# One added VectorE sum in place of a second ones product for key group 3, its product moved behind the next q/k product, and GpSimd's bias passes moved in its order

## The chip, the cores and the metric

The kernel runs on one core of a Trainium2 chip. The metric is the device time in microseconds (us) of one execution; lower is better. TensorE multiplies matrices, VectorE and ScalarE work on up to 128 partitions elementwise, GpSimd (POOL in the rows) is a third elementwise engine, SyncE issues most of the transfers (DMA). Each engine runs its own list of instructions in order and waits on semaphores for the others.

## The reference, cut to what matters

A decoder layer over a batch of 16 sequences, 256 positions, 512 channels, all in float32:

```
x = _layernorm(x + attention(x))          # 16 heads of 32, softmax over the keys, low-rank updates folded into the weights
x = _layernorm(x + x * scan(ctx * ctx))   # a decaying sum over positions: r = d * r + ctx * ctx
x = _layernorm(x + ffn(x))                # rms_norm, 8-bit activations, ternary weights, 512 -> 2048 -> 512
# inside the ffn: silu, gelu, layer_norm with gain and bias, then quantised again
```

The softmax needs, for each head and query, the sum of exp(score) over the 256 keys. The kernel gets it as a product of the exponentials with a block of ones, beside the product with the values.

## The kernel before

The 16 batches are software-pipelined. Each engine has a lead, then `body(j)` for j = 1 to 15, then a drain. `body(j)` holds work on several batches: attention of batch j (four groups c = 0 to 3 of four heads each), the output product, first two layer norms and first FFN product of batch j-1, the middle of the FFN (gelu, norm, gain, bias, quantisation: called z) of batch j-2, the second FFN product and last norm of batch j-3. The names end in their batch: `quantise_z(j - 2, 0)` works on the first half (q = 0) of the 256 positions of batch j-2. The order inside a body is written out by hand per engine, and the semaphore counts in `table` join the engines.

What the change and the steps of the prediction touch:

- Attention. `probs` (128 keys x 2 key halves x 4 heads x 256 queries, float32) is written by ScalarE in `probs_of(b, c)` (L657, two instructions). TensorE's `weighted(b, c)` makes the product with the values (L1406, 16 small matmuls) and the product with `ones` (L1415, 16 matmuls, for c = 1 to 3). For c = 0, VectorE adds the two key halves first (`add_halves`, L979, into `half_sum`, which lies over `x_round`), and the ones product has 8 matmuls (L1411). VectorE's `attn_norm(b, c)` (L993 to L1002) waits for `pv_ready`, the count of finished ones products, and divides. `maxima` (L963) reduces the scores to maxima.
- z path. GpSimd `h_rstd` (L534 to L540), ScalarE `h_norm` (L740), GpSimd `g_mul` (L549, the gain), VectorE `z_add` (L1094, the bias), `z_max` (L1099) and `quantise_z` (small steps L1117 to L1123, then the large L1126), ScalarE `zq_store` (L710). Behind `zq_store(j - 2, 0)` in ScalarE's list come the eight `silu` of batch j-1 (L719), which empty the PSUM banks of TensorE's first FFN product `f(j, u)`, u = 0 to 7 (L1482 and L1483). Three banks take turns, so `f(j, 3)` waits for the first `silu`. After the eighth come two `gelu` (L725), the next body's `probs_of(j, 0)`, `h_var` (L735) and `h_norm`.
- Scan. VectorE `scan(j)` (L1010, four instructions of 128x256, then L1013) is the last item of VectorE's body.
- GpSimd's bias passes. `res1(b)` (L498, two of 128x512) adds the output bias to the rows of x, `res2(b)` (L507, the same size) the FFN's. Both stand at the head of GpSimd's body: `res1(j - 1)`, `res2(j - 2)`, `neg_mean` (L527) twice, `inverse_std3`, `h_rstd`.
- `normalise(3, b, q)` (L695) is ScalarE's last norm of a batch before it is stored. SyncE's body: load xT, `transpose_z(j - 3, 1)`, `store_out(j - 3, 0)`, `load_ctx`, `transpose_x(j - 1)`, `store_out(j - 3, 1)`, `transpose_z(j - 2, 0)`, `load_rows(j)`.

Of the kernel before, what the change touches and what calls it, by code (L numbers as in the profile page):

```python
# [12 lines left out]
ALU = mybir.AluOpType  # L13
# [4 lines left out]
T = 256  # L18
# [29 lines left out]
def decoder_kernel(nc, x, xT, ctxT, W, L, bq, bk, bv, bo, decay, w1T, b1, ln_g, ln_b, w2T, b2, out):  # L48
    b1_scratch = nc.dram_tensor("b1_scratch", (NPART, INNER), BF16, kind="Internal").ap()

    with ExitStack() as ctx:
# [70 lines left out]
        def sem(name):  # L122
# [40 lines left out]
            (PE, "shiftT_ready", 4), (PE, "pv_ready", 4), (PE, "o_ready", 2), (PE, "rT_ready", 2),  # L163
# [8 lines left out]
            (DV, "half_added", 1), (DV, "qk_lo", 8), (DV, "max_done", 4), (DV, "shift_split", 8), (DV, "inverted", 12), (DV, "attn_done", 4),  # L172
# [101 lines left out]
        def _(sp):  # L274
# [83 lines left out]
            def body(j):  # L358
# [6 lines left out]
                transpose_x(j - 1)  # L365
                if alive(j, 3):
                    store_out(j - 3, 1)
                if alive(j, 2):
                    transpose_z(j - 2, 0)
                load_rows(j)  # L370
# [38 lines left out]
        def _(po):  # L409
# [162 lines left out]
            attn_split(0, 3)  # L572

            def body(j):
                if alive(j, 1):
                    res1(j - 1)
                if alive(j, 2):
                    res2(j - 2)
                    neg_mean(j - 2, 0)
                    neg_mean(j - 2, 1)  # L580
# [27 lines left out]
                if alive(j, 2):  # L608
                    z_rms(j - 2, 1)

            def drain():
                res1(LAST)
# [32 lines left out]
        def _(ac):  # L645
# [162 lines left out]
            def body(j):  # L808
# [54 lines left out]
                if alive(j, -1):  # L863
                    v_store(j + 1, 0)
                if alive(j, 0):
                    probs_of(j, 3)
# [4 lines left out]
                if alive(j, 3):  # L871
                    normalise(3, j - 3, 1)
# [71 lines left out]
        def _(dv):  # L944
# [30 lines left out]
            def add_halves(b):  # L975
# [3 lines left out]
                dv.tensor_tensor(half_sum, probs[:, 0, :, :], probs[:, 1, :, :], ALU.add).then_inc(S["half_added"], 1)  # L979

# [206 lines left out]
            def lead():  # L1187
# [28 lines left out]
                maxima(1, 0)  # L1216
                attn_norm(0, 3)
# [5 lines left out]
            def body(j):  # L1223
# [42 lines left out]
                if alive(j, 2):  # L1266
                    z_add(j - 2, 1)
                    quantise_z(j - 2, 0)
# [54 lines left out]
        def _(pe):  # L1323
# [72 lines left out]
            def weighted(b, c):  # L1396
# [6 lines left out]
                for kt in range(NT):  # L1403
                    for i in range(GH):
                        ch = (GH * c + i) * HD
                        pe.matmul(bank[4][i * HD:(i + 1) * HD, 0:T], v_sb[b % 2][:, kt, ch:ch + HD], probs[:, kt, i, :],  # L1406
                                  start=(kt == 0), stop=(kt == NT - 1))
                if c == 0:
                    wait(pe, "half_added", b, 1)
                    for i in range(GH):  # L1410
                        last = pe.matmul(bank[4][i * HD:(i + 1) * HD, T:2 * T], ones[:, :], half_sum[:, i, :],  # L1411
                                         start=True, stop=True)
                for kt in range(NT if c > 0 else 0):
                    for i in range(GH):
# [314 lines left out]
```

## Time and profile before

| | |
|---|---|
| median of 3 runs | 1043.13 us (1042.7 to 1046.71) |
| the profiled execution | 1045.01 us, its span 1043.2 us |
| clock granted to TensorE over the span | 0.961 of full speed |
| core of the pipeline | bodies 3 to 15, a batch each 57.6 us |
| lead and first bodies | up to about 224 us of the span |
| drain | from about 960 us |

The span is the stretch between first and last instruction in the profile. A row of a timeline gives start, duration, engine, line, operation, what it writes and reads, and in brackets how long the engine sat idle just before, and for whom. The chain of waits follows the work that ended last back from the end. "issue" in it is time in which the profile shows nothing that the engine waited for.

### The profile page before, as it was taken

How to read it: one execution, taken by the hardware profiler on the slowest of the kernel's cores; microseconds unless marked ns; L12 is line 12 of the kernel's file. 1: busy time of each engine (PE TensorE's matmuls, PEld its weight loads, DVE VectorE, ACT ScalarE, POOL GpSimd, SP SyncE). 2: the span in 40 equal slices, each digit the busy share in tenths (PEclk: the TensorE clock that was granted, in tenths of full speed). 3: DMA queues.
4: the chain of work that ended last, by engine and by line, in shares of the span. 5: the costliest groups of instructions: out<-in, count | busy, mean ns of one | idle time of the engine just before them, and what ended most of it. 6: DMA issues, size and time to landing. Idle time of an engine off the chain costs nothing.

```text
span 1043.2 us, 23326 instructions
## 1 busy us (share of the span) xinstructions
PE 945.8 (91%) x9260; PEld 647.9 (62%) x9260; DVE 909.1 (87%) x1490; ACT 827.8 (79%) x957; POOL 582.7 (56%) x767
## 2 busy tenths in 40 slices
PE   4898897999999999999999999999999999977415
PEld 3776656676776667676767767676767777654102
DVE  5577878999999999999999999999999999996766
ACT  3556686888889797988989797989889897978684
POOL 3322338374765748484747658484747566572653
PEclk8899998999999999999999999999999999999768
DMA  9423100313122122323132121323131222122214
GB/s 361 156 87 137 43 33 21 74 34 99 25 58 70 49 75 52 84 52 85 21 85 52 55 62 52 84 52 85 52 85 22 71 61 58 42 52 63 53 33 90
DMA packets 106351, 73.67 MB, mean 71 GB/s; under 512 B 91385, under 2 KB 91385, under 8 KB 104450
## 3 DMA queue, kind: packets, MB, share of 16 engines
q1 hardware_dynamic: 105522, 70.34, 24.7%
q8 instruction: 74, 1.21, 0.5%
q10 hardware_dynamic: 720, 1.84, 0.5%
q14 instruction: 35, 0.29, 0.1%
HBM read 41.73 MB, written 8.40 MB: 48 GB/s over the span
## 4 chain that ended last, share of the span: by engine, by line
DVE 32%; PE 29%; ACT 16%; issue 13%; POOL 7%; DMA 3%; SPq 1%; DVEq 0%; ACTq 0%; POOLq 0%
PE bank L1343 9%; PE bank L1482 8%; DVE neg_max L963 6%; POOL h L549 5%; ACT h L725 3%; DVE h L1094 3%; DVE stats L1020 3%; ACT junk L735 2%; ACT h L740 2%; DVE qk_parts L986 2%; DVE fz L1099 2%; PE bank L1483 2%; PE wave L1392 2%; ACT L725 2%; PE wave L1368 2%
## 5 line engine op out<-in xcount | busy, mean ns | idle before, releaser
L963 DVE TENSOR_REDUCE neg_max<-wave 128x8 f32<-128x2048 f32 x64 | 146.1, 2282 | 20.0 <-PE wave L1368 20.0
L549 POOL TENSOR_TENSOR h<-h,g_tile 128x2048 f32<-128x2048 f32 x30 | 139.8, 4660 | 39.1 <-ACT h L740 39.1
L657 ACT ACTIVATE probs<-wave 128x1024 f32<-128x1024 f32 x128 | 124.3, 1024 | 37.8 <-PE wave L1392 37.7
L1482 PE MATMUL bank<-w,xqT 128*128 128x512 fp8e4 x496 | 130.0, 385 | 15.8 <-DMA xqT<-xq 13.0
L439 POOL TENSOR_SCALAR attn_hi<-attn 128x256 fp32r<-128x256 f32 x64 | 28.1, 439 | 176.4 <-DVE attn L1002 161.5
L695 ACT ACTIVATE rows<-rows,rstd 128x512 f32<-128x512 f32 x96 | 74.3, 807 | 41.1 <-POOL rstd L455 23.6
L1094 DVE TENSOR_TENSOR h<-h,b_tile 128x2048 f32<-128x2048 f32 x32 | 84.1, 2630 | 18.6 <-POOL h L549 18.0
L719 ACT ACTIVATE h<-bank,qx 128x512 f32<-128x512 f32 x124 | 82.3, 689 | 19.8 <-PE bank L1483 17.8
L498 POOL TENSOR_TENSOR rows<-rows,bo_tile 128x512 f32<-128x512 f32 x32 | 57.2, 1809 | 71.6 <-DMA rows<-x 71.6
L1489 PE MATMUL bank<-w,hqT 128*128 128x512 fp8e4 x416 | 94.3, 380 | 0.5 <-DMA hqT<-h 0.5
L1482 PEld LDWEIGHTS bank<-w,xqT 128*128 128x128 bf16 x496 | 46.6, 99 | 74.7 <-DMA xqT<-xq 9.9
L1010 DVE TENSOR_TENSOR_SCAN ctx_sb<-decay_col,ctx_sb 128x256 f32<-128x256 f32 x64 | 89.5, 1457 | 0.0
L1343 PE MATMUL bank<-xT_hi,wq_hi 128*128 128x256 f32 x256 | 77.8, 304 | 0.1
L1392 PE MATMUL wave<-qk_parts 32*128 32x256 f32 x1536 | 74.2, 302 | 3.8 <-ACT shift_rows L679 3.8
L442 POOL TENSOR_TENSOR attn_lo<-attn,attn_hi 128x256 fp32r<-128x256 f32 x64 | 73.5, 1148 | 5.3
L740 ACT ACTIVATE h<-h,fs 128x2048 f32<-128x2048 f32 x32 | 66.8, 2090 | 10.8 <-POOL fs L540 10.8
L672 ACT ACTIVATE qk_parts<-bank,bias_qk 128x256 fp32r<-128x256 f32 x128 | 53.6, 474 | 25.4 <-PE bank L1343 25.4
L1406 PE MATMUL bank<-probs,v_sb 128*32 128x256 f32 x1024 | 70.9, 396 | 3.1 <-ACT probs L657 2.1
L1392 PEld LDWEIGHTS wave<-qk_parts 32*128 32x128 f32 x1536 | 57.5, 190 | 25.8 <-issue 18.9
L1368 PE MATMUL wave<-qk_parts 32*128 32x256 f32 x1536 | 63.8, 297 | 10.1 <-ACT probs L657 8.0
L1343 PE MATMUL bank<-xT_lo,wq_hi 128*128 128x256 f32 x256 | 72.8, 284 | 0.0
L1343 PE MATMUL bank<-xT_hi,wq_lo 128*128 128x256 f32 x256 | 72.6, 284 | 0.0
(184 smaller groups left out, 2817.9 us busy)
## 6 DMA issues: line engine op xcount, KB each, us to landing
ctx_sb<-ctxT SPq DMA_DIRECT2D x16, 512.0 KB, 3.7
rows<-x SPq DMA_DIRECT2D x16, 512.0 KB, 4.0
out<-rows SPq DMA_DIRECT2D x32, 256.0 KB, 2.5
xT_in<-xT SPq DMA_DIRECT2D x15, 512.0 KB, 4.7
h<-w1T SPq DMA_DIRECT2D x4, 1024.0 KB, 14.3
h<-w2T SPq DMA_DIRECT2D x4, 1024.0 KB, 4.8
h<-Wq SPq DMA_DIRECT2D x1, 1024.0 KB, 6.0
h<-Wk SPq DMA_DIRECT2D x1, 1024.0 KB, 9.7
```

The source lines that it names most:

```text
L549: po.tensor_tensor(h_of(b, q)[:, :], h_of(b, q)[:, :], g_tile[:, :], ALU.mult).then_inc(done, 1)
L657: ac.activation(probs[:, kt, :, :], wave[:, :, kt * T:(kt + 1) * T], ACT.Exp, scale=SM_SCALE).then_inc(S["probs_ready"], 1)
L719: ac.activation(h_of(b, q)[:, n * FW:(n + 1) * FW], bank_of("f", u, b), ACT.Silu, scale=qx[:, X_DEQ, q:q + 1]).then_inc(S["silu_done"], 1)
L740: ac.activation(h_of(b, q)[:, :], h_of(b, q)[:, :], ACT.Identity, scale=fs[:, q, H_RSTD:H_RSTD + 1], bias=fs[:, q, H_NB:H_NB + 1]).then_in ...
L963: dv.tensor_reduce(neg_max[:, :, :], wave[:, :, :].rearrange("p j (t k) -> p j t k", t=NT), axis=AX_X, op=ALU.max, negate=True).then_inc(S ...
L1010: dv.tensor_tensor_scan(ctx_sb[:, c, :], decay_col[:, c:c + 1].to_broadcast([P, T]), ctx_sb[:, c, :], 0.0, ALU.mult, ALU.add).then_inc(S[" ...
L1094: dv.tensor_tensor(h_of(b, q)[:, :], h_of(b, q)[:, :], b_tile[:, :], ALU.add).then_inc(S["z_added"], 1)
L1343: last = pe.matmul(psum, lhsT, rhs, start=(first and i == 0), stop=(final and i == len(pairs) - 1))
L1368: last = pe.matmul(bank[head][:, qt * T:(qt + 1) * T], parts[at, qp, qt * P:(qt + 1) * P], parts[at, kp, :], start=(i == 0), stop=(i == 2))
L1392: last = pe.matmul(bank[head][:, kt * T:(kt + 1) * T], keys, queries, start=(i == 0), stop=(i == 3))
L1482: pe.matmul(p[:, :], xqT[:, q, kc, :], w1[:, kc, n * FW:(n + 1) * FW], start=(kc == 0), stop=False)
L1489: last = pe.matmul(p[:, :], hqT[:, k, :], w2[:, k, :], start=(k == 0), stop=(k == FC - 1))
```

## The change

- `weighted(b, 3)` makes only the product with the values, and counts it on a new semaphore `values_ready`. VectorE's new `add_in_place(b)` waits for it, adds `probs[:, 0]` to `probs[:, 1]` in place, 128x1024 float32, and counts `half_added`. The ones product of group 3, `summed(b, 3)`, then has 8 matmuls where it had 16, and stands behind `qk(j + 1, 1)`. Groups 0 to 2 keep their products and their places.
- `add_in_place(j)` stands in VectorE's body between `z_add(j - 2, 1)` and `quantise_z(j - 2, 0)`.
- On GpSimd `res1(j)` moves to the end of body j, behind a wait for `shift_split` of batch j+1 (its first `maxima`). `res2(j - 2)` now waits for the scan of batch j-1, behind `neg_mean(j - 2, 0)`.
- On ScalarE `normalise(3, j - 3, 1)` moves up, ahead of `probs_of(j, 3)`. On SyncE `store_out(j - 3, 1)` moves ahead of `transpose_x(j - 1)` and `load_rows(j)` ahead of `transpose_z(j - 2, 0)`.

```diff
--- before.py
+++ after.py
@@ -160,7 +160,7 @@
         table = [
 
             (PE, "shifted_ready", 4), (PE, "scores_ready", 4), (PE, "qk_ready", 4), (PE, "v_ready", 2),
-            (PE, "shiftT_ready", 4), (PE, "pv_ready", 4), (PE, "o_ready", 2), (PE, "rT_ready", 2),
+            (PE, "shiftT_ready", 4), (PE, "pv_ready", 4), (PE, "values_ready", 1), (PE, "o_ready", 2), (PE, "rT_ready", 2),
             (PE, "f_ready", 8), (PE, "y_ready", 2),
 
             (AC, "probs_ready", 8), (AC, "v_stored", 2), (AC, "x_hi", 1), (AC, "qk_hi", 8),
@@ -169,7 +169,7 @@
             (AC, "xq_stored", 1), (AC, "silu_done", 8), (AC, "zq_stored", 2),
             (AC, "gelu_done", 2), (AC, "h_var", 2), (AC, "h_normed", 2), (AC, "z_squared", 2),
 
-            (DV, "half_added", 1), (DV, "qk_lo", 8), (DV, "max_done", 4), (DV, "shift_split", 8), (DV, "inverted", 12), (DV, "attn_done", 4),
+            (DV, "half_added", 2), (DV, "qk_lo", 8), (DV, "max_done", 4), (DV, "shift_split", 8), (DV, "inverted", 12), (DV, "attn_done", 4),
             (DV, "scan_done", 5), (DV, "ln1", 6), (DV, "ln2", 6), (DV, "x_quant", 14),
             (DV, "z_added", 4), (DV, "z_quant", 12),
             (DV, "ln3", 6),
@@ -362,12 +362,12 @@
                     transpose_z(j - 3, 1)
                     store_out(j - 3, 0)
                 load_ctx(j)
-                transpose_x(j - 1)
                 if alive(j, 3):
                     store_out(j - 3, 1)
+                transpose_x(j - 1)
+                load_rows(j)
                 if alive(j, 2):
                     transpose_z(j - 2, 0)
-                load_rows(j)
 
             def drain_transpose(b, q):
 
@@ -570,13 +570,13 @@
             attn_split(0, 1)
             attn_split(0, 2)
             attn_split(0, 3)
+            res1(0)
 
             def body(j):
-                if alive(j, 1):
-                    res1(j - 1)
-                if alive(j, 2):
+                if alive(j, 2):
+                    neg_mean(j - 2, 0)
+                    wait(po, "scan_done", j - 1, 5)
                     res2(j - 2)
-                    neg_mean(j - 2, 0)
                     neg_mean(j - 2, 1)
                 if alive(j, 3):
                     inverse_std3(j - 3, 0)
@@ -607,9 +607,11 @@
                     attn_split(j, 3)
                 if alive(j, 2):
                     z_rms(j - 2, 1)
+                if alive(j, -1):
+                    wait(po, "shift_split", j + 1, 2)
+                res1(j)
 
             def drain():
-                res1(LAST)
                 neg_mean(PRIOR, 0)
                 neg_mean(PRIOR, 1)
                 inverse_std1(LAST)
@@ -862,14 +864,14 @@
                     shiftT(j, 3)
                 if alive(j, -1):
                     v_store(j + 1, 0)
+                if alive(j, 3):
+                    normalise(3, j - 3, 1)
                 if alive(j, 0):
                     probs_of(j, 3)
                 if alive(j, 1):
                     xq_store(j - 1)
                 if alive(j, -1):
                     v_store(j + 1, 1)
-                if alive(j, 3):
-                    normalise(3, j - 3, 1)
                 if alive(j, 0):
                     ctx_square(j)
                 if alive(j, 2):
@@ -978,6 +980,13 @@
                 wait(dv, "xq_stored", b - 2, 1)
                 dv.tensor_tensor(half_sum, probs[:, 0, :, :], probs[:, 1, :, :], ALU.add).then_inc(S["half_added"], 1)
 
+            def add_in_place(b):
+
+                wait(dv, "probs_ready", b, 8)
+                wait(dv, "values_ready", b, 1)
+                dv.tensor_tensor(probs[:, 1, :, :], probs[:, 0, :, :], probs[:, 1, :, :],
+                                 ALU.add).then_inc(S["half_added"], 1)
+
             def qk_lo(b, c):
 
                 wait(dv, "qk_hi", b, 2 * (c + 1))
@@ -1214,6 +1223,7 @@
                 attn_norm(0, 2)
                 ternary(1)
                 maxima(1, 0)
+                add_in_place(0)
                 attn_norm(0, 3)
                 qk_lo(1, 1)
                 ternary(2)
@@ -1265,6 +1275,8 @@
                     quantise_x(j - 1)
                 if alive(j, 2):
                     z_add(j - 2, 1)
+                add_in_place(j)
+                if alive(j, 2):
                     quantise_z(j - 2, 0)
                 if j == 1:
                     ternary(7)
@@ -1403,17 +1415,26 @@
                 for kt in range(NT):
                     for i in range(GH):
                         ch = (GH * c + i) * HD
-                        pe.matmul(bank[4][i * HD:(i + 1) * HD, 0:T], v_sb[b % 2][:, kt, ch:ch + HD], probs[:, kt, i, :],
-                                  start=(kt == 0), stop=(kt == NT - 1))
-                if c == 0:
-                    wait(pe, "half_added", b, 1)
+                        last = pe.matmul(bank[4][i * HD:(i + 1) * HD, 0:T], v_sb[b % 2][:, kt, ch:ch + HD],
+                                         probs[:, kt, i, :], start=(kt == 0), stop=(kt == NT - 1))
+                if c == 3:
+                    last.then_inc(S["values_ready"], 1)
+                else:
+                    summed(b, c)
+
+            def summed(b, c):
+
+                if c in (0, 3):
+                    wait(pe, "half_added", b, 1 if c == 0 else 2)
+                    both = half_sum if c == 0 else probs[:, 1, :, :]
                     for i in range(GH):
-                        last = pe.matmul(bank[4][i * HD:(i + 1) * HD, T:2 * T], ones[:, :], half_sum[:, i, :],
+                        last = pe.matmul(bank[4][i * HD:(i + 1) * HD, T:2 * T], ones[:, :], both[:, i, :],
                                          start=True, stop=True)
-                for kt in range(NT if c > 0 else 0):
-                    for i in range(GH):
-                        last = pe.matmul(bank[4][i * HD:(i + 1) * HD, T:2 * T], ones[:, :], probs[:, kt, i, :],
-                                         start=(kt == 0), stop=(kt == NT - 1))
+                else:
+                    for kt in range(NT):
+                        for i in range(GH):
+                            last = pe.matmul(bank[4][i * HD:(i + 1) * HD, T:2 * T], ones[:, :], probs[:, kt, i, :],
+                                             start=(kt == 0), stop=(kt == NT - 1))
                 last.then_inc(S["pv_ready"], 1)
 
 
@@ -1600,6 +1621,7 @@
                 scores(1, 0)
                 weighted(0, 3)
                 qk(1, 1)
+                summed(0, 3)
                 shiftT(1, 0)
                 shifted(1, 0)
 
@@ -1663,6 +1685,7 @@
                     weighted(j, 3)
                 if alive(j, -1):
                     qk(j + 1, 1)
+                summed(j, 3)
                 if j == 1:
                     pe.wait_ge(u_tern, 4)
                     pe.wait_ge(u_b1_in, 16 * NPART)
```

## Rows read from the trace of the kernel before

**Rows 1.** The page's busy time, share of the span and instructions of each engine.
```profile
PE 945.8 (91%) x9260; PEld 647.9 (62%) x9260; DVE 909.1 (87%) x1490; ACT 827.8 (79%) x957; POOL 582.7 (56%) x767
```

**Rows 2.** One batch's stretch: length, busy PE, PEld, DVE, ACT, POOL, clock, DMA.
```profile
627.20:684.80 57.60, 57.05 (x579) 39.48 (x578) 53.61 (x90) 49.34 (x59) 36.12 (x48) 1.00 0.25 62
```

**Rows 3.** Chain of waits, 627 to 687 us: start, us, what.
```profile
627.31 1.84 DVE h L1094
...
654.22 1.30 DVE h L1126
655.57 2.00 issue
659.60 1.04 PE bank L1482 x4
...
674.59 1.98 ACT junk L735 x2
678.04 2.11 ACT h L740
680.22 4.69 POOL h L549
684.93 1.80 DVE h L1094
```

**Rows 4.** Timeline of VectorE, 593 to 630 us.
```profile
593.44 2.29 DVE L1094 TENSOR_TENSOR h<-h,b_tile 128x2048 f32<-128x2048 f32 x1
595.65 0.15 DVE L1117 TENSOR_TENSOR fz<-fz 128x1 f32<-128x1 f32 x1
...
607.80 6.66 DVE L1010 TENSOR_TENSOR_SCAN ctx_sb<-decay_col,ctx_sb 128x256 f32<-128x256 f32 x4
...
618.24 1.21 DVE L979 TENSOR_TENSOR x_round<-probs 128x1024 f32<-128x1024 f32 x1
619.37 2.28 DVE L963 TENSOR_REDUCE neg_max<-wave 128x8 f32<-128x2048 f32 x1
...
627.31 2.48 DVE L1094 TENSOR_TENSOR h<-h,b_tile 128x2048 f32<-128x2048 f32 x1 [1.38 <-POOL h L549]
```

**Rows 5.** Who waited for whom: us in total, times, longest.
```profile
DVE h L1094 <- POOL h L549: 18.0, 13, 1.4
```

**Rows 6.** Timeline of ScalarE: body 2, then 597 and 647 us.
```profile
196.38 1.28 ACT L719 ACT_TABLE_LOAD   x1 [0.32 <-PE bank L1483]
...
597.99 2.00 ACT L710 ACTIVATE h<-h,neg_round 128x2048 bf16<-128x2048 f32 x1 [0.22 <-DVE h L1126]
...
647.48 1.95 ACT L657 ACTIVATE probs<-wave 128x1024 f32<-128x1024 f32 x2 [0.51 <-PE wave L1392]
```

**Rows 7.** Timeline of TensorE, 594 to 620 us.
```profile
594.56 1.05 PE L1415 MATMUL bank<-probs,ones 128*32 128x256 f32 x16
...
602.05 1.04 PE L1482 MATMUL bank<-w,xqT 128*128 128x512 fp8e4 x4 [0.17 <-ACT h L719]
...
619.89 0.61 PE L1411 MATMUL bank<-x_round,ones 128*32 128x256 f32 x8
```

**Rows 8.** Timeline of GpSimd, 599 to 620 us.
```profile
599.58 0.40 POOL L439 TENSOR_SCALAR attn_hi<-attn 128x256 fp32r<-128x256 f32 x1 [8.47 <-DVE attn L1002]
...
606.81 3.84 POOL L498 TENSOR_TENSOR rows<-rows,bo_tile 128x512 f32<-128x512 f32 x2 [5.11 <-DMA rows<-x]
610.61 3.30 POOL L507 TENSOR_TENSOR rows<-rows,b_tile 128x512 f32<-128x512 f32 x2
...
619.08 0.42 POOL L534 TENSOR_SCALAR fs<-fs 128x1 f32<-128x1 f32 x1 [1.01 <-ACT junk L735]
```

**Rows 9.** All instructions of L1010 and of L498: ns minimum/median/maximum.
```profile
L1010 DVE TENSOR_TENSOR_SCAN ctx_sb<-decay_col,ctx_sb x64: 659/1693/1784, 86.8 to 951.4; 128x256 f32<-128x256 f32 x64
...
L498 POOL TENSOR_TENSOR rows<-rows,bo_tile x32: 1261/1656/2350, 79.8 to 953.9; 128x512 f32<-128x512 f32 x32
```

**Rows 10.** Timeline of VectorE in the lead, 80 us.
```profile
80.07 0.87 DVE L986 SCALAR_TENSOR_TENSOR qk_parts<-bank,bias_qk,qk_parts 128x256 fp32r<-128x256 f32 x2 [1.49 <-ACT qk_parts L672]
```

## The prediction, made before the changed kernel ran

> **What bounds the kernel now.** I read the page's busy shares first. TensorE is busy 945.8 us of the span and VectorE 909.1 [rows 1], which names two candidates and decides nothing. The view by stretches comes next. A batch of the steady part takes 57.60 us, and in it TensorE is busy 57.05, VectorE 53.61, ScalarE 49.34 and GpSimd 36.12 [rows 2]. TensorE has half a microsecond of air, so a loop that is longer than 57.05 and runs through several engines must set the period. The chain of waits shows it [rows 3]. The reader is to see the same item, `z_add` of the first half (L1094), at 627.31 and again at 684.93, 57.62 us later, and what lies between.
>
> First comes a stretch of VectorE alone, from `z_add(j-2, 0)` at 627.31 to the end of `quantise_z(j-2, 0)` (L1126) at 655.5, some 28.2 us. Then the chain leaves VectorE: `zq_store` on ScalarE (the 2.00 us called issue at 655.57), a table load, the first `silu`, TensorE's `f(j, 3)` at 659.60 and the four after it, the last `silu`, both `gelu`, `probs_of`, `h_var` at 674.59, GpSimd's `h_rstd`, `h_norm` at 678.04, `g_mul` of 4.69 us, and again `z_add` [rows 3]. Each joint is tight. `zq_store` started 0.22 us after it was free, on VectorE's L1126 [rows 6]. `f(j, 3)` came after 0.17 us of idle TensorE, on the first `silu` [rows 7]. `h_rstd` came after 1.01 us of idle GpSimd, on `h_var` [rows 8]. `z_add(j-2, 0)` came after 1.38 us of idle VectorE, on `g_mul` [rows 4], and that wait occurs 13 times, 18.0 us in all [rows 5].
>
> So VectorE's list falls into two parts of unlike value. Between `z_add(j-2, 0)` and `quantise_z(j-2, 0)` each microsecond is a microsecond of the period. Between `quantise_z(j-2, 0)` and the next `z_add` (last group's division, `maxima`, scan, norms, `add_halves`) VectorE has 1.38 us in hand, and time saved there only lengthens the wait for `g_mul`.
>
> **The change part by part.**
>
> The new sum on VectorE. It stands between `z_add(j-2, 1)` and `quantise_z(j-2, 0)`, in the part without slack. Its twin is `add_halves` (L979), the same 128x1024 float32 with both inputs in SBUF: 1.21 us, and the next item starts 619.37 - 618.24 = 1.13 us after it [rows 4]. The neighbours here overlap in the same way (L1094 of 2.29 us, next start 2.21 later), so I take 1.13. That it writes over an input isn't shown by any row; I see no work removed or added by it. What it waits for has happened: `z_add(j-2, 1)` ends at 595.7, and the product with the values ends just after 594.6, where the ones product starts [rows 4, 7]. Behind it wait `quantise_z`, and through it `zq_store`, all eight `silu` and TensorE's `f(j, 3)`. ScalarE is free before L1126 ends [rows 6], so nothing covers it: +1.13 a batch, at most 1.21.
>
> The ones product on TensorE. 16 matmuls took 1.05 us [rows 7], 8 take 0.61: 0.44 saved in front of `f(j, 0)`, and `qk(j+1, 1)` starts some 0.9 earlier. It lies ahead of `f(j, 3)`, which waits for the first `silu`. TensorE's idle time of 0.17 there becomes 0.17 + 0.44 + 1.13 = 1.74 us. Worth nothing while the loop binds. `summed(j, 3)` needs the sum at about 596.9 and TensorE reaches it after `qk` at 597.5, so no stall. `f(j, 2)` uses the bank of the last group's division, which is now 1.13 later, near 600.7, about where `f(j, 2)` stood: a few tenths, ahead of the same wait.
>
> GpSimd's passes and the scan. Beside the bias passes (3.84 and 3.30 us) the scans took 6.66 us [rows 4, 8]. Over all batches one scan has a minimum of 0.66 and a median of 1.69, one bias pass a minimum of 1.26 and a median of 1.66 [rows 9]. With the passes gone I expect 4 x 0.66 less overlap, some 2.4 to 2.6 us: 4.2 saved. The scan stands in the part of VectorE with slack, so the wait before `z_add` grows from 1.38 to about 5.5 and the period gains nothing. What is late next is still `g_mul`.
>
> The two waits that this adds on GpSimd. `res1(j)` waits for the first `maxima` of batch j+1 at the very end of the body, with nothing queued behind it but `neg_mean(j-1, 0)`, due after a `gelu` some 8 us later. It then runs beside `z_max`, from about 603.2 to 605.8. `res2` waits for the scan with `neg_mean(j-2, 1)`, `inverse_std3` and then `h_rstd` behind it, and `h_rstd` is in the loop. The scan with its clip would end at 607.8 + 1.1 + 2.4 + 0.7 = 612.0, two passes of 1.26 to 1.7 end by 615.5, and 1.5 us of small steps bring GpSimd to 617. `h_rstd` is due at 619.08 + 1.13 = 620.2. Cost nothing, with 3 us in hand; bounds 0 and 1.5 (rival below).
>
> ScalarE's `normalise(3, j-3, 1)`, 0.8 us, goes ahead of `probs_of(j, 3)`, which sat idle 0.51 us for TensorE [rows 6]. The exponentials come 0.3 later; they end near 591.8 and are read at 593.7. No cost. SyncE's `store_out` ahead of `transpose_x` costs about 0.7 us of issue if both are due at once, but the norm it waits for now comes 3 us earlier. `load_rows` no longer stands behind the transposes of z, so x arrives some 7 us earlier (it was what GpSimd waited 5.11 us for [rows 8]). The transposed x has about 1 us before `f(j, 0)`, and behind that the 1.74 of `f(j, 3)`. Nothing.
>
> A rule against the row. The rows say that scans next to GpSimd's passes last two and a half times as long. The Trainium skill, page "SBUF — State Buffer", section "Who interferes with whom", says why: VectorE's second read port is GpSimd's, and whoever comes first holds it for the whole instruction. The trace agrees with the lengths. By that rule the new sum, which has two SBUF inputs, could itself be held up by a GpSimd pass. GpSimd sat idle for 8.47 us up to 599.58 [rows 8], so I add nothing for it.
>
> First bodies. In the lead VectorE waits 1.49 us for `qk_hi(1, 1)` [rows 10]. The sum fits in it, but the last ones product now comes behind `qk(1, 1)`, and `attn_norm(0, 3)` with it, so `qk_lo(1, 1)` slips by about 0.4 us. In body 1 TensorE is the chain and gains 0.44. Together 0, bounds -0.9 and +1.4. In body 2 ScalarE had 0.32 us of idle time on TensorE behind `zq_store` [rows 6]: +1.13 - 0.32 = +0.8. Bodies 3 to 15, 13 of them, cost 1.13 each: 14.7. The drain starts from the same chain and does the same work: 0.
>
> Sum: 0 + 0.8 + 14.7 = +15.5 us. Against the profiled execution that is 1045.0 + 15.5 = 1060.5. That execution lies 1.9 above the median of the runs, which the forecast follows: 1043.1 + 15.5 = **1058.6 us**, 1.5% slower.
>
> **The rivals.**
>
> A, not slower, the loop is not the bound. If VectorE's own list or TensorE's set the period, the sum would be paid from the scan's 4.2 us, and TensorE's 0.44 would show: 57.60 to about 57.05 - 0.44 = 56.6, some -1.0 x 13 = 1030 us; with TensorE alone binding, 1043.1 - 13 x 0.44 = 1037. For it: TensorE is busy 57.05 of 57.60, and the scan is the largest single saving. Against it: the 1.38 us of idle VectorE before `z_add` in each of 13 batches, and 0.17 before `f(j, 3)`. It decides only if the loop had over 1.13 us of slack; the rows leave it none. 5%.
>
> B, half of it covered. The stretch on VectorE holds some lengthening beside GpSimd: L1094 of 2.48 against 2.29 us [rows 4], and I allow as much again for the smaller items. If the new order frees these, some 0.4 us come off: 13 x 0.7 + 0.8 - 0.9 (lead) = 9.0, 1052. 8%.
>
> C, slower still: the wait of `res2` for the scan takes the place of what was removed. If the scan stays at 6.66 us, because other GpSimd work lands on it, it ends at 616.3, `res2` at 3.3 us ends at 619.6, the small steps at 621.1, and `h_rstd` is 0.9 late; together with a late x it may be 1.5: 1058.6 + 13 x 0.9 to 1.5 = 1070 to 1078. It decides from 3 us of delay on GpSimd. Against it: GpSimd has nothing else to do between the end of `res1` and the scan's end. 9%.
>
> **How the numbers follow.** The forecast has 78%, B 8%, C 9%, A 5%. The forecast's own bounds: at most 14 x 1.21 + 1.4 = 18.3 and 2 to 3 us for the spread of the runs (1042.7 to 1046.7), so 1065; below, down to B's 1052. The range is 1052 to 1065; it leaves out A and C, 14%, and some of the forecast's tail. A measurement here can tell about 0.5% (5 us) from no change. Slower by more than that: forecast, C and most of B, 92%. Within 0.5%: 4%. Faster: 4%.
>
> **What the profile after would show.** Right: 58.7 us from one `z_add(j-2, 0)` to the next; four scans in about 2.5 us; VectorE idle some 5 us before L1094, on `g_mul`; ScalarE idle 1.3 us before `zq_store`; TensorE idle over a microsecond before `f(j, 3)`; the new sum in the chain of waits. Wrong for A: TensorE without gaps and a period of 57.1 or less. For C: GpSimd's `h_rstd` starts on its own queue, not on `h_var`. For B: a shorter VectorE stretch but for the sum. What would make the prediction wrong is a joint of the loop that the new order shortens, between `zq_store` and `g_mul` above all, and I see none.

## The result, and the profile after

The changed kernel takes **1060.12 us**, median of 4 runs (1059.41 to 1061.78), against 1043.11 us for the kernel before in the same comparison: ratio 1.0158, 95% interval 1.0144 to 1.0171. It is 1.6% slower. The prediction said 1058.6. By the medians the change costs 17.0 us, where the prediction's sum had +15.5. The two profiled executions (1060.42 and 1045.01 us) lie 15.4 apart, but that of before is 1.9 above its median and that of after 0.3 above its own.

The page's busy row, and one batch by the view of stretches (columns as in rows 2):

```profile
PE 948.3 (90%) x9116; PEld 645.6 (61%) x9132; DVE 878.2 (83%) x1506; ACT 826.1 (78%) x957; POOL 549.0 (52%) x767
```
```profile
227.40:286.10 58.70, 57.01 (x586) 39.30 (x580) 51.32 (x92) 49.41 (x59) 33.61 (x48) 1.00 0.24 61
```

Beside [rows 1] VectorE lost 31 us of busy time, 2 a batch, and GpSimd 34, and yet the kernel is slower. The length of the stretch, 58.70 us, was chosen; the batches themselves take 58.5, about 0.9 more than in before (table below), and all of it is idle time. The chain of waits of after (start, us, what), to be laid beside [rows 3]:

```profile
601.22 1.39 DVE h L1103
...
603.43 1.22 DVE probs L987
...
605.59 1.30 DVE h L1135
...
606.93 2.00 issue
608.93 1.28 ACT L721
...
610.97 1.04 PE bank L1503 x4
...
625.95 1.98 ACT junk L737 x2
...
631.31 4.71 POOL h L549
636.04 1.78 DVE h L1103
```

The new sum (L987) stands in the chain between `z_add(j-2, 1)` and `quantise_z(j-2, 0)`; behind it come `zq_store` (called issue), the `silu`, `f(j, 3)`, `h_var`, `g_mul` and the next `z_add(j-2, 0)`, the same joints as before. In other batches (659.73) the profile's chain passes over ScalarE's square of `z_add`'s result in place of the sum. The two end within hundredths of each other there, and by the code `quantise_z(j - 2, 0)` waits for the square of its own half only, done long before.

VectorE's timeline of the same batch (start, us, line, operation, out<-in, and in brackets the idle time before it and what ended it):

```profile
601.22 2.29 DVE L1103 TENSOR_TENSOR h<-h,b_tile 128x2048 f32<-128x2048 f32 x1
603.43 1.22 DVE L987 TENSOR_TENSOR probs<-probs 128x1024 f32<-128x1024 f32 x1
...
616.72 2.43 DVE L1019 TENSOR_TENSOR_SCAN ctx_sb<-decay_col,ctx_sb 128x256 f32<-128x256 f32 x4
...
621.50 0.75 DVE L1148 SCALAR_TENSOR_TENSOR rows<-bank,fz,rows 128x512 f32<-128x512 f32 x1 [1.63 <-PE bank L1510]
...
624.27 0.69 DVE L1037 TENSOR_TENSOR rows<-bank,rows 128x512 f32<-128x512 f32 x1 [1.06 <-PE bank L1355]
...
628.05 2.29 DVE L965 TENSOR_REDUCE neg_max<-wave 128x8 f32<-128x2048 f32 x1 [0.84 <-PE wave L1380]
...
636.04 2.48 DVE L1103 TENSOR_TENSOR h<-h,b_tile 128x2048 f32<-128x2048 f32 x1 [1.43 <-POOL h L549]
```

The four scans fell from 6.66 us [rows 4] to 2.43. Those 4.2 us became idle time of VectorE, but not where the prediction had put it. Only 1.43 us lie before `z_add` (1.38 before); 1.63, 1.06 and 0.84 lie further up, before three items whose input comes from TensorE. The reader should note these three brackets: they show that VectorE's list behind the scan is tied to TensorE three times before it is tied to `g_mul`. That matters in experiments 4 and 5.

GpSimd, and ScalarE's `zq_store`:

```profile
611.11 2.50 POOL L498 TENSOR_TENSOR rows<-rows,bo_tile 128x512 f32<-128x512 f32 x2 [0.49 <-DVE shift L975]
...
621.03 2.55 POOL L507 TENSOR_TENSOR rows<-rows,b_tile 128x512 f32<-128x512 f32 x2
...
628.00 0.19 POOL L534 TENSOR_SCALAR fs<-fs 128x1 f32<-128x1 f32 x1 [2.99 <-ACT junk L737]
```
```profile
606.91 2.00 ACT L712 ACTIVATE h<-h,neg_round 128x2048 bf16<-128x2048 f32 x1 [1.36 <-DVE h L1135]
```

### The profile page after: what moved, and what is told of

Its sections match the earlier page's. It is cut to its first block, busy times and chain, and to the rows that moved or that the text cites. A ratio compares the mean times of both kernels' runs of the same rounds, so it can differ in the third digit from the quotient of the medians.

```text
span 1058.6 us, 23113 instructions
## 1 busy us (share of the span) xinstructions
PE 948.3 (90%) x9116; PEld 645.6 (61%) x9132; DVE 878.2 (83%) x1506; ACT 826.1 (78%) x957; POOL 549.0 (52%) x767
## 4 chain that ended last, share of the span: by engine, by line
DVE 36%; PE 23%; ACT 20%; issue 12%; POOL 8%; DMA 2%; SPq 0%; DVEq 0%; ACTq 0%; POOLq 0%
PE bank L1503 8%; PE bank L1355 6%; DVE neg_max L965 6%; POOL h L549 6%; DVE h L1103 5%; ACT h L727 3%; ACT h L742 3%; ACT junk L737 3%; DVE stats L1029 3%; ACT junk L752 2%; DVE fz L1108 2%; DVE qk_parts L995 2%; ACT L727 2%; PE bank L1504 2%; ACT L659 2%
## 5 line engine op out<-in xcount | busy, mean ns | idle before, releaser
L1503 PE MATMUL bank<-w,xqT 128*128 128x512 fp8e4 x496 | 131.3, 388 | 28.5 <-ACT h L721 16.9
L1103 DVE TENSOR_TENSOR h<-h,b_tile 128x2048 f32<-128x2048 f32 x32 | 84.1, 2629 | 18.9 <-POOL h L549 18.4
L752 ACT ACTIVATE junk<-h 128x2048 bf16<-128x2048 f32 x32 | 61.1, 1910 | 21.3 <-DVE h L1103 21.3
L712 ACT ACTIVATE h<-h,neg_round 128x2048 bf16<-128x2048 f32 x30 | 59.8, 1997 | 18.9 <-DVE h L1135 18.9
L1355 PE MATMUL bank<-xT_hi,wk_hi 128*128 128x256 f32 x256 | 72.4, 283 | 0.0
```

The lines of the kernel that those rows point to most:

```text
L752: ac.activation(junk[:, :], h_of(b, q)[:, :], ACT.Square, accum_out=fs[:, q, H_ZSS:H_ZSS + 1]).then_inc(S["z_squared"], 1)
L1103: dv.tensor_tensor(h_of(b, q)[:, :], h_of(b, q)[:, :], b_tile[:, :], ALU.add).then_inc(S["z_added"], 1)
L1355: last = pe.matmul(psum, lhsT, rhs, start=(first and i == 0), stop=(final and i == len(pairs) - 1))
L1503: pe.matmul(p[:, :], xqT[:, q, kc, :], w1[:, kc, n * FW:(n + 1) * FW], start=(kc == 0), stop=False)
```

## The experiments

Two theories stood at the outset. T1, the prediction's: one loop (`z_add`, sum, `quantise_z(0)`, `zq_store`, `silu`, `f(3)` to `f(7)`, `gelu`, `h_var`, `g_mul`) sets the period, a microsecond of VectorE inside it is a microsecond of each batch, and outside it is free. The rival: what costs time is something else that came with the change (the new order of GpSimd and of the queues, the late product of ones, the write in place).

For the time of one batch, the table takes the start of `g_mul` in the trace of each kernel, from `g_mul(1, 0)` at the head of body 3 (218.78 us in before) to `g_mul(13, 0)` at the head of body 15 (911.23), and divides by the 12 batches between them. The marks are the same items in every kernel. The last column is the median of the 12 single steps.

| kernel | median us | ratio, 95% interval | us a batch, mean | median step |
|---|---|---|---|---|
| before | 1043.11 | | 57.70 | 57.58 |
| after | 1060.12 | 1.0158 (1.0144 to 1.0171) | 58.52 | 58.49 |
| e1 moves only | 1041.09 | 0.9976 (0.9965 to 0.9987) | 57.42 | 57.33 |
| e2 sum only | 1061.33 | 1.0176 (1.0155 to 1.0197) | 58.68 | 58.68 |
| e3 work in the loop | 1058.63 | 1.0143 (1.0119 to 1.0167) | 58.76 | 58.69 |
| e4 work off the loop | 1057.21 | 1.0136 (1.0115 to 1.0156) | 58.77 | 58.79 |
| e8 as e4, with the moves | 1040.43 | 0.9970 (0.9954 to 0.9986) | 57.40 | 57.36 |
| e5 sum in batches 2 to 14 | 1056.87 | 1.0121 (1.0098 to 1.0144) | 58.52 | 58.49 |
| e6 loop shorter, no sum | 1038.22 | 0.9939 (0.9920 to 0.9958) | 57.16 | 57.00 |
| e10 the same again | 1039.86 | 0.9947 (0.9926 to 0.9969) | 57.12 | 57.07 |
| e7 as e6, with the sum | 1045.21 | 1.0009 (0.9995 to 1.0022) | 57.62 | 57.57 |
| e9 as e7, `z_add` later | 1056.31 | 1.0113 (1.0092 to 1.0135) | 58.45 | 58.40 |

The steps aren't all alike. In before four of the 12 are longer than the median by 0.35 to 0.6 us, in after one, in e1 two, in e2 none. In three of the four a small step of VectorE on 128x2 (L1064 or L1065, usually 0.17 us) took 0.62 to 0.65, in the fourth GpSimd's L534 took 0.78. The medians leave them out, and by them the sum costs the same with and without the moves: 1.16 us (after against e1) and 1.10 (e2 against before). The ratios are each against before in the same comparison; before itself had medians from 1042.98 to 1044.68 us in the four comparisons.

**1. The moves alone (e1_moves_only).** After, without the new sum: group 3's product of ones is again 16 matmuls in `weighted`.

```diff
-                if c == 3:
-                    last.then_inc(S["values_ready"], 1)
-                else:
-                    summed(b, c)
+                summed(b, c)
-                add_in_place(j)
-                summed(j, 3)
```

> The changed kernel without its new sum: group 3 keeps its 16 ones matmuls in their old place, while the moves on GpSimd, ScalarE and SyncE stay. Theory T (the whole loss is the sum, which stands on the loop through zq_store, silu, gelu, h_rstd and g_mul): the period falls back to 57.6 us or a little under it, since the small steps of h_rstd no longer share VectorE's port and took 0.2 us less in the changed kernel: 1040 to 1043 us. Rival W (the new waits on GpSimd or the early loads cost the time): 1055 to 1060 us.

Measured: 1041.09 us, and a batch of 57.42: the moves are no cost, and the two waits on GpSimd and the new order of the queues hurt nothing. They are even a gain, small but outside the interval. Its place is in GpSimd's `h_rstd`. In before, the first small step of `h_rstd` (L534 in [rows 8], 0.42 us from 619.08) ended at 619.50, and VectorE's sum (L979 in [rows 4]) at 619.45. In e1, as in after, VectorE is past that sum when `h_var` is done, and the step takes 0.19 us:

```profile
616.75 0.19 POOL L534 TENSOR_SCALAR fs<-fs 128x1 f32<-128x1 f32 x1 [2.99 <-ACT junk L737]
```

0.23 us a batch out of the loop is nearly all of the 0.25 between the median steps (57.58 and 57.33). The pair with the sum agrees: L534 takes 0.38 to 0.41 us in e2 and 0.19 in after, and the median steps are 58.68 and 58.49. The cause, GpSimd's small step held while VectorE's sum runs, is read from the two ends that coincide; no run changed it alone. The Trainium skill, page "SBUF — State Buffer", section "Who interferes with whom", has the same reading: a VectorE instruction with two SBUF inputs contends with a GpSimd instruction that reads SBUF, for a port pair that only one of them holds at a time.

**2. The sum alone (e2_sum_only).** Before, with `add_in_place`, `values_ready` and the late product of ones, and none of the moves.

```diff
                 if alive(j, 2):
                     z_add(j - 2, 1)
+                add_in_place(j)
+                if alive(j, 2):
                     quantise_z(j - 2, 0)
```

> The kernel before with only the new sum and the late product of ones for group 3; GpSimd, ScalarE and SyncE keep the old order. Theory T: 1.13 us a batch in bodies 3 to 14, 0.9 in body 2, and what the changed kernel lost in body 1 and at the end (1.8 and 2.6 us): about 1062 us, 2 to 3 us above the changed kernel. Rival W: about 1043 us.

Measured: 1061.33 us, 58.68 a batch, +0.98 by the mean and +1.10 by the median step; 1.2 us above after, where 2 to 3 were expected. The whole loss is there without any move. The rival "it came with the moves" is out.

**3. The same VectorE work in the loop, nothing else (e3_work_in_loop).** TensorE, the counts and `probs` are as in before. VectorE adds two constant tiles into a spare tile at the sum's place (the output is bfloat16, the time 1.22 us as the sum's). This work is idle work; the result doesn't use it.

```diff
+            def extra(j):
+                if j >= 3:
+                    dv.tensor_tensor(spare[:, :], g_tile[:, 0:1024], b_tile[:, 0:1024], ALU.add)
...
                     z_add(j - 2, 1)
+                    extra(j)
                     quantise_z(j - 2, 0)
```

> The kernel before with one more VectorE addition of 128x1024 float32 from two constant tiles into an unused tile (no reader, the result is the same), between z_add(j-2, 1) and quantise_z(j-2, 0), in bodies 3 to 15. Nobody waits for it and TensorE is untouched. Theory T: it costs its 1.13 us of VectorE time in each of 13 bodies, 14.7 us: about 1058 us. If instead the waits of the sum or its late product are what costs: under 1048 us.

Measured: 1058.63 us, 58.76 a batch, +1.06. Neither the write over an input, nor the wait for the values, nor the late product is needed for the loss in the steady batches: this VectorE work of 1.22 us at the same place is enough. What e2 has beyond it (2.7 us) is, by the traces, in the first bodies (1.6) and in the drain (1.4).

**4. The same work off the loop (e4_work_off_loop).** `extra(j)` goes behind the scan, where T1 has 1.38 us in hand.

```diff
                 scan(j)
+                extra(j)
```

> The same extra addition in the same 13 bodies, but behind the scan at the end of VectorE's body, in the part where VectorE has 1.38 us in hand before z_add(j-2, 0). Theory T: 1.13 fits in 1.38, the wait for g_mul shrinks to 0.2 to 0.3 us, 1043 to 1045 us. If VectorE's list as a whole were the bound (rival A of the prediction): about 1058 us, as with the extra work in the loop.

Measured: 1057.21 us, 58.77 a batch. T1 missed by 12 us. The place that was to be free costs as much as the loop. From VectorE's timeline the wait for `g_mul`, and behind it the chain of waits:

```profile
634.53 2.48 DVE L1100 TENSOR_TENSOR h<-h,b_tile 128x2048 f32<-128x2048 f32 x1 [1.09 <-POOL h L550]
```
```profile
614.28 6.58 DVE ctx_sb L1016 x4
...
621.49 1.22 DVE spare L985
...
626.89 2.29 DVE neg_max L964
...
629.64 0.44 PE wave L1384 x2
630.08 1.40 PE bank L1350 x6
...
638.44 3.58 PE bank L1496 x16
642.04 0.76 DVE rows L1145
```

The chain doesn't go through `g_mul` here. It goes scan, extra work, the norms, `maxima(j, 1)`, then to TensorE's `shiftT(j, 1)` (629.64), through 12.4 us of TensorE's list to the second FFN product (L1496), from there back to VectorE, which adds it to the rows (L1145 at 642.04), and down VectorE's list to `quantise_z(j-2, 0)`, `zq_store`, the first `silu`, `qk_hi`, `qk_lo`, `quantise_z(j-2, 1)` and the next scan at 673.05, 58.77 us after this one. And `z_add` still waits 1.09 us for `g_mul`. So in before there was a **second loop** with almost no slack: the 1.22 us (1.13 of it after overlap) cost 1.07 by the mean and 1.21 by the median step. The new sum's place, ahead of `quantise_z(j-2, 0)`, lies on both loops. The 1.38 us before `z_add` never were slack of VectorE's list; they are the distance between two arrivals at that one item, and the list was already bound further up, through `shiftT`. That is theory T2.

**5. T2 tested (e8_off_loop_moved).** The extra work again behind the scan, but with the moves of e1, in which the scan is 4.2 us shorter. T2 says it is now hidden, for the second loop is shorter by 4.2.

> The kernel of the moves alone (group 3 with its 16 ones matmuls) plus the same extra VectorE addition behind the scan in bodies 3 to 15. In the kernel before this addition cost 14 us, against my expectation. Theory T2 (there is a second loop, from the silu through qk_hi, qk_lo, quantise_z of the second half, the scan, the layer norm sums and maxima(j, 1) to TensorE's shiftT, with under 0.2 us of slack in the kernel before; the moves shorten it by the scan's 4.2 us): the addition is now hidden, 1041 to 1042 us. Rival A2 (VectorE's time costs wherever it stands): 1055 us.

```profile
603.54 2.43 DVE L1018 TENSOR_TENSOR_SCAN ctx_sb<-decay_col,ctx_sb 128x256 f32<-128x256 f32 x4
...
606.61 1.22 DVE L987 TENSOR_TENSOR spare<-g_tile,b_tile 128x1024 bf16<-128x1024 f32 x1
608.32 0.75 DVE L1147 SCALAR_TENSOR_TENSOR rows<-bank,fz,rows 128x512 f32<-128x512 f32 x1 [0.49 <-PE bank L1504]
```

Measured: 1040.43 us, 57.40 a batch, against 57.42 in e1: hidden whole. The item behind the extra work (L1147) still waits 0.49 us for TensorE; in e1 its twin waits 1.63, so the work took 1.14 of idle time. So the same instruction at the same place costs 1.07 us a batch beside the long scans and nothing beside the short ones. The changed kernel did free the second loop, and the first, which the moves don't shorten by more than 0.25 us, paid for the sum.

**6. The edges (e5_sum_in_2_to_14).** After, with `ADDED = range(2, 15)`: batches 0, 1 and 15 have their 16 matmuls back.

> The changed kernel with the new sum only for batches 2 to 14; batches 0, 1 and 15 keep the 16 ones matmuls in their old place. Theory T: the two edges go, 1.8 us in body 1, where the sum delayed the last ternary weights, and some 2.6 us at the end, where TensorE waited 4.3 us for the sum and came back at half its clock: 1055 to 1056 us. If the edges are not where these came from: 1059 to 1060 us.

Measured: 1056.87 us, 3.25 below after by the medians, just above the expected range. The two profiled executions differ less, 1060.42 and 1058.97: that of e5 is the slowest of its four runs. By the traces, the first `g_mul` starts at 155.28 (155.18 in before, 156.97 in after). These starts contain the lead, which scatters: `add_halves(1)`, near the head of VectorE's body 1, starts at 88.58 us in e6 and 91.86 in e10, which are one kernel. From that item to the first `g_mul` are 63.7 us in before, e3, e4, e5, e6, e8 and e10 (64.6, 65.3 and 64.6 in e1, e7 and e9) and 65.9 in both kernels that have the sum there, after and e2. So against the usual 63.7 the sum costs 2.2 us in body 1. In body 1 of after the sum waits for the values, and the ternary weights queue behind it (here VectorE's timeline):

```profile
128.84 1.23 DVE L987 TENSOR_TENSOR probs<-probs 128x1024 f32<-128x1024 f32 x1 [2.02 <-PE bank L1418]
129.99 1.28 DVE L1157 TENSOR_SCALAR h<-h,w_scale 128x2048 f32<-128x2048 f32 x1
```

At the other end the sum in body 15 makes TensorE stand still, since there is no `qk(16)` in front of its product. The granted clock falls to 0.50 in the idle time, and the first products of `f` run at this lower level. In before TensorE stands still at this place too, for the transposed x, and its first four matmuls of `f` are also at 0.50 (TensorE's timelines of after, then of before; four such matmuls take 1.03 us at the upper level):

```profile
955.09 1.08 PE L1431 MATMUL bank<-probs,ones 128*32 128x256 f32 x8 [4.31 <-DVE probs L987]
956.10 1.89 PE L1503 MATMUL bank<-w,xqT 128*128 128x512 fp8e4 x4
```
```profile
942.62 1.86 PE L1482 MATMUL bank<-w,xqT 128*128 128x512 fp8e4 x4 [3.57 <-DMA xqT<-xq]
```

From the `g_mul` before it (923.72) to this first `f` are 32.4 us, against 31.4 in before (911.23 to 942.62) and 31.4 in e5: the sum costs 1.0 there. But e5 gains nothing from it: its third four matmuls of `f` are still at the lower level (1.85 us; 1.34 in after, 1.03 in before), and its y product takes 6.59 us (6.35 in after, 5.31 in before). Of the 2.8 us that after loses from there to the end, about 1.0 is the sum and the rest is time at the lower level, which e5 has too without the sum. In e2, with the same sum, the shift in body 15 is 1.1 us and comes to 2.6 only in the drain. When the level returned differs between kernels by microseconds; no run here settles why.

**7. The first loop made shorter (e6_loop_shorter).** From e1, two items leave the loop: `z_add(j-2, 1)` goes behind `quantise_z(j-2, 0)`, and ScalarE's square of it behind the first `silu`.

```diff
                 if alive(j, 2):
-                    z_add(j - 2, 1)
                     quantise_z(j - 2, 0)
+                    z_add(j - 2, 1)
...
+                    if u == 0 and 1 <= b < LAST:
+                        z_square(b - 1, 1)
```

> The kernel of the moves alone, with quantise_z(j-2, 0) ahead of z_add(j-2, 1) on VectorE and the square of the second half behind the first silu on ScalarE. This takes 2.2 us out of the first loop. Theory T: the loop was the bound by half a microsecond over TensorE's own work of 57.05 us a batch, so TensorE becomes the bound and the period falls from 57.35 to 57.0 or 57.1: 1037 to 1039 us. If the loop as I read it is not what binds: 1041 us or slower.

Measured: 1038.22 us, 0.9939 of before, and again on another chip, as e10_loop_shorter_again, 1039.86 us and 0.9947. It is faster than both kernels. The view of stretches over 57 us:

```profile
571.50:628.50 57.00, 56.65 (x577) 39.58 (x577) 49.99 (x91) 48.92 (x59) 33.39 (x48) 1.00 0.25 63
```

TensorE is busy 56.65 of 57.00 with VectorE at 49.99, and its waits for the `silu` before `f(3)` (1.3 us in four waits between 300 and 870 us in e1) are gone. So TensorE is nearly the bound. What idle time it has lies mainly before L1479, the product that brings in the scan's result, where it waits up to 0.3 us for VectorE's `rows`. 2.2 us of VectorE left the loop and 0.26 came off the batch; the rest met TensorE's list. The 57.05 us of busy TensorE in before, which the prediction and this expectation used as TensorE's own work, was no floor: the same matmuls are busy 56.8 us in e1 and 56.65 here.

**8. The sum where it should be free (e7_sum_beside).** From e6, with the sum of batches 2 to 14 between `quantise_z(0)` and `z_add(1)`. By then I held that the sum is outside both loops, and that TensorE, being the bound, would pay back its 8 matmuls.

```diff
                     quantise_z(j - 2, 0)
+                add_in_place(j)
                     z_add(j - 2, 1)
```

> As the last one, but with the new sum for batches 2 to 14, between quantise_z(j-2, 0) and z_add(j-2, 1), so off the loop, and TensorE with 8 matmuls less a batch. Theory T: the sum is hidden on VectorE; TensorE's work is 56.6 us a batch, but f(j, 2) waits some 0.4 us for the division of the last group, so 56.7 to 57.0: 1033 to 1038 us, faster than both kernels. If TensorE waits for the sum or for the late square: 1041 us or more.

Measured: 1045.21 us, 57.62 a batch: 0.46 to 0.50 more than e6 and e10, in place of less, and 7 us above the expected range. TensorE didn't pay anything back either: it is busy 56.9 us a batch with 8 matmuls fewer. The chain of waits:

```profile
652.16 1.22 DVE probs L992
653.38 2.20 DVE h L1108
...
657.03 2.29 DVE neg_max L967
...
659.79 0.44 PE wave L1394 x2
660.22 0.86 PE bank L1508 x4
```

A third path: sum, `z_add(1)`, last group's division, `maxima(j+1, 0)`, and TensorE's `shiftT(j+1, 0)`, which stands between `f(3)` and `f(4)` and waits 0.28 us here.

**9. That path cleared (e9_sum_behind_maxima).** From e7, `z_add(j-2, 1)` moves behind `maxima(j+1, 0)`, the square behind the fifth `silu`.

```diff
                 add_in_place(j)
-                    z_add(j - 2, 1)
...
                     maxima(j + 1, 0)
+                    z_add(j - 2, 1)
                     z_max(j - 2, 1)
```

> The kernel of e7_sum_beside with one thing moved: on VectorE z_add(j-2,1) no longer stands between the sum and maxima(j+1,0), it follows maxima(j+1,0), and ScalarE's z_square(j-2,1) follows the silu of unit 4 in place of that of unit 0. The sum of batches 2 to 14 stays. Theory T3 (e7 lost 7 us because the sum and z_add stood ahead of maxima(j+1,0), and the transposes of the scales, which stand on TensorE between f(3) and f(4), wait for those maxima): maxima(j+1,0) comes some 2.2 us earlier than in e7, TensorE has no idle time in a period again, period 56.6 to 57.0 us, 1034 to 1038 us in all. Rival (the sum costs wherever it stands in this order, because VectorE's 1.22 us are then missing at the next thing TensorE waits for, or the later square delays the last silus): period 57.3 or more, 1041 us or more.

> The kernel of e6_loop_shorter once more (no sum; quantise_z(j-2,0) ahead of z_add(j-2,1), z_square(j-2,1) behind the first silu), on the chip of e9_sum_behind_maxima, so that the two can be set side by side: 1035 to 1040 us, ratio 0.992 to 0.996. If T3 holds, the kernel with the sum is at or up to 2 us below this one, since 24 fewer products of ones a batch leave TensorE; if the rival holds, it is 3 us or more above.

Measured, on one chip: 1056.31 us with it, 1039.86 for e10 without the sum. T3 missed by 18 us, and the rival's side of the expectation came. (The 24 products of ones in it are a slip: the sum removes 8 matmuls a batch.) From VectorE's timeline the wait of the last group's division, then the chain of waits:

```profile
661.61 0.45 DVE L1007 STREAM_TRANSPOSE sums_T<-bank 128x256 f32<-128x256 f32 x1 [1.55 <-PE bank L1435]
```
```profile
660.97 0.61 PE bank L1435 x8
...
663.15 2.29 DVE neg_max L967
...
665.85 2.21 DVE h L1108
...
671.17 1.17 DVE fz L1131
...
672.75 0.81 DVE fz L1134
...
673.83 1.29 DVE h L1140
675.12 2.36 DVE ctx_sb L1024 x4
677.50 0.70 DVE ctx_sb L1027
678.28 2.54 POOL rows L508 x2
...
681.33 1.55 POOL rstd L488
...
683.60 0.56 POOL fs L538
...
684.45 2.11 ACT h L745
686.62 4.65 POOL h L550
```

The premise of T3 failed first. `maxima(j+1, 0)` (663.15) starts 5.5 us behind `quantise_z(0)`, where e7 had 6.1, so 0.6 us came off in place of 2.2. The division ahead of it now waits 1.55 us for the product of ones (L1435), which stands behind `qk(j+1, 1)` and is late (22.7 us in 14 waits). So here the product's new place costs time, which it didn't do in the steady batches of after. TensorE's waits at the `shiftT` between `f(3)` and `f(4)` are no shorter than in e7 (2.7 us in ten, 2.5 in nine, from 300 to 870 us). And `z_add(1)` and `z_max(1)` have landed in front of `quantise_z(1)` and the scan. The scan releases GpSimd's `res2` (the wait that the change added: 33.4 us in 13 waits, up to 2.6 each), and behind `res2` queues `h_rstd`. That is a fourth path, and it is the prediction's rival C, met in another kernel: GpSimd runs from `res2` at 678.28 to the end of `h_rstd` at 684.4 without a gap, so `h_rstd` starts when its queue is free and not when `h_var` is done. Three small steps on this path are held up beside the other engine's work: VectorE's L1131 and L1134 take 1.16 and 0.80 us in place of 0.16 beside GpSimd's `res1`, GpSimd's L488 takes 1.54 in place of 0.56 beside VectorE's `add_halves`. Together that is 2.6 us of a batch that is 1.3 longer than in e10; no run took it away. Two things moved at once here (the `z_add` and the square), so what T3 says of the third path is neither shown nor refuted; what is shown is that this order has another one.

## Why the prediction was right, point by point

**What bounds the kernel: half right.** The loop through `z_add`, `quantise_z(0)`, `zq_store`, `f(3)` and `g_mul` is the bound, and work in it costs 1.06 (e3) to 1.10 us (after against e1) of a predicted 1.13, by the median steps 1.11 and 1.16. VectorE's stretch from `z_add(j-2, 0)` to the end of `quantise_z(j-2, 0)` grew from 28.20 to 29.4 us. The claim that VectorE's other part had 1.38 us in hand is false: e4 paid 1.07 or more of 1.13. In before this part belongs to a second loop of nearly the same length. The false claim did no harm to the forecast only because the same change took 4.2 us off that part. Rival A was put aside with this wrong argument, though its rejection stands: the first loop alone was enough.

**The terms**, by the shift of `g_mul` between the traces of before and after. In brackets is the start of the first `g_mul` behind that stretch; the measured number is what the shift grew by since the row above:

| stretch | predicted | measured |
|---|---|---|
| lead and body 1 | 0 | +1.8 (155.18 to 156.97) |
| body 2 | +0.8 | +0.9 (218.78 to 221.44) |
| bodies 3 to 14 | 12 x 1.13 = 13.6 | +9.8 (911.23 to 923.72) |
| body 15 | +1.1 | +2.5 (981.91 to 996.92) |
| drain | 0 | +0.3 (1009.73 to 1025.02) |
| sum | +15.5 | +15.3 |

The total agrees better than its terms do; that is partly luck. It hides an exchange: alone, the sum with its late product costs 18.4 us (e2), and the moves, priced at nothing, give back 1.9 (e1). And by the medians the shift is 17.0, not 15.3. **Steady bodies**: 0.82 each. The sum's 1.13 was sized right (next start 604.57 - 603.43 = 1.14), but the loop also became shorter by 0.23 in `h_rstd`, which leaves the 0.91 between the median steps. The other 0.09 is the irregular long batches, four in before and one in after, and no run shows that it belongs to the change. The prediction's own words name the step, "a joint of the loop that the new order shortens, between `zq_store` and `g_mul` above all, and I see none". It was to be seen: the row of L534 at 0.42 us in [rows 8], with the sum of [rows 4] running beside it. **Body 1**: the price of 0 was wrong, and so its bound of +1.4. From `add_halves(1)` on body 1 costs 2.2 us, and 0.4 of that is hidden by a lead that happened to be shorter. The text saw the product behind `qk(1, 1)` but not the sum's wait of 2.02 us for the values with ternary work queued behind it. **Body 15**: the cover named for the late product was `qk(j+1, 1)`, and body 15 has none; the prediction said what hides the product and didn't ask where that cover is missing. Some 1.0 us is that wait, the rest time at the lower clock level. **Drain**: about right.

**The scan**: predicted 2.4 to 2.6, measured 2.43. **The bias passes** beside the shorter scans: 1.25 and 1.28 us each, within 1.26 to 1.7 but for a hundredth. **Rival C's margin**: "3 us in hand" for `h_rstd`, measured 2.99 idle before it. **ScalarE before `zq_store`**: predicted 1.3, measured 1.36. **TensorE before `f(3)`**: predicted over 1 (1.74 by the sum), measured 1.25 (14 such waits, 16.9 us in all):

```profile
610.97 1.04 PE L1503 MATMUL bank<-w,xqT 128*128 128x512 fp8e4 x4 [1.25 <-ACT h L721]
```

**VectorE's idle time**: the amount was near (4.96 against "about 5.5"), the place wrong, as shown above. **Held up by GpSimd**: the new sum took 1.216 to 1.225 us in all 16 batches, so nothing held it, as the prediction assumed from [rows 8]. **TensorE's 0.44** didn't show as less busy time: 56.8 us a batch in e1 and in after.

**Rival B** (+9.0 by overlap on VectorE) isn't what happened, though 9.8 in the steady bodies looks like it: the sum's own cost was whole, and the gain came on GpSimd. At 0.82 a batch its mechanism would have had to show in VectorE's stretch, which is longer by the sum's whole 1.14.

## What to carry to other kernels

An idle time in front of one item tells how far apart its two inputs arrive, and not how much slack the engine's list has. To find slack, follow every item of the list that another engine waits for, and ask for each how late it may be; in a pipeline tuned until TensorE is 99% busy, expect more than one loop of nearly the same length. Here there were two within about 0.1 us, and two more paths came up when the order changed (e7 and e9). A gain in one is worth only the distance to the next.

When work is hidden behind an item of the next batch, ask what happens in the first and the last batch, where that item isn't there.

## What was not expected of the hardware

GpSimd's [128x1] step of 0.19 us took 0.42 beside a VectorE sum with two SBUF inputs and ended with it. Small steps in a critical loop can be held up by a neighbour, not only the long passes. In e9 it went the other way too: a VectorE step on 128x1 took 1.16 us in place of 0.16 beside a GpSimd pass. The scans show the same at size: 1.69 us (median) beside GpSimd's passes in before [rows 9], 0.66 to 0.69 in all 64 instructions of after.

After 4.3 us of idle TensorE and the 8 matmuls of the late product, four fp8 matmuls of 512 columns took 1.89 us at a granted clock of 0.50, against 1.03 at 1.00. In before they took 1.86 after 3.6 us of idle time. The level came back during the second group of four in before, during the third in after and at the end of the third in e5, so that a few microseconds at the end of the kernel shift from one kernel to the next without any change in the work there.
